# Attention and expert block on one core: unit 15's scores, mask and exponential take other places in their engines' orders

## The reference

```
x = x + attention(layernorm(x))     # 16 heads of 64, causal, with a second layernorm inside
x = x + experts(layernorm(x))       # encoder, router, 2 of 8 experts, decoder, layernorm
```

```
scores = jnp.where(causal, einsum('bqhe,bkhe->bhqk', q, k) * scale, -inf)
z = einsum('bhqk,bkhe->bqhe', softmax(scores, axis=-1), v)
attn_out = einsum('bqhe,hed->bqd', z, W_o) + b_o
```

## Time and profile before

| what | us |
|---|---|
| median of 3 runs | 1162.31 |
| the runs | 1160.6 to 1169.64 |
| the profiled execution, its time | 1161.35 |
| its span, first to last instruction | 1159.6 |
| busy in it: TensorE, VectorE, ScalarE, GpSimd | 1033.9, 861.9, 739.5, 743.9 |
| one attention step, 414.20 to 443.31 | 29.11 |

### The profile page before, as it was taken

One profiled execution on the slowest core, in us unless ns is written; L12 is line 12 of the kernel. 1 busy time (PEld: TensorE's weight loads), 2 busy tenths in 40 slices (PEclk: granted clock), 3 DMA queues, 4 the chain that ended last, 5 costly groups with the idle time before them and its releaser, 6 DMA issues.

```text
span 1159.6 us, 51488 instructions
## 1 busy us (share of the span) xinstructions
PE 1033.9 (89%) x19852; PEld 768.7 (66%) x19852; DVE 861.9 (74%) x2047; ACT 739.5 (64%) x1540; POOL 743.9 (64%) x728
## 2 busy tenths in 40 slices
PE   5789999999999999999999999999999978899984
PEld 2567777777777777777777777777777766454542
DVE  7877777777777777777777777777777786357563
ACT  4656666666666666666666666666666655667663
POOL 5786666666666666666666666666666633344544
PEclk8999999999999999999999999999999998899998
DMA  7678877777777777777777777777777773131322
GB/s 172 160 192 210 195 181 186 184 185 186 183 183 187 187 182 188 185 184 184 185 185 184 186 183 184 186 183 186 184 183 186 188 149 76 38 83 47 91 59 51
DMA packets 131599, 188.79 MB, mean 163 GB/s; under 512 B 46576, under 2 KB 57840, under 8 KB 131568
## 3 DMA queue, kind: packets, MB, share of 16 engines
q1 hardware_dynamic: 131568, 188.40, 67.9%
HBM read 133.39 MB, written 21.36 MB: 133 GB/s over the span
## 4 chain that ended last, share of the span: by engine, by line
PE 65%; POOL 13%; issue 8%; DVE 6%; ACT 5%; DMA 1%; POOLq 1%; DVEq 0%; ACTq 0%; SPq 0%
PE ZB L714 27%; PE SPS L697 13%; PE SPS L698 10%; POOL QS L495 6%; PE ZB L687 5%; POOL X L520 3%; POOL QS L493 3%; ACT RAW L1279 2%; ACT OT L1316 1%; PE SPS L849 1%; PE SPS L875 1%; PE ZB L681 1%; PE ZB L890 1%; PE ZB L884 1%; ACT PRL L1299 1%
## 5 line engine op out<-in xcount | busy, mean ns | idle before, releaser
L1018 DVE CUSTOM_DVE_ANT_0 SSB<-SPS,MASK 128x640 f32<-128x640 f32 (+7 forms) x512 | 375.1, 751 | 174.5 <-PE SPS L698 163.6
L714 PE MATMUL ZB<-PTZ,VR 32*64 32x256 f32 (+2 forms) x16384 | 321.5, 294 | 30.9 <-ACT RAW L1279 23.7
L697 PE MATMUL SPS<-KHP,QS 128*128 (+2 forms) x768 | 323.5, 427 | 23.9 <-DVE NM L1018 19.5
L1299 ACT ACTIVATE PRL<-SSB,NM 128x640 f32<-128x640 f32 (+3 forms) x256 | 253.1, 989 | 128.4 <-DVE NM L1018 128.0
L714 PEld LDWEIGHTS ZB<-PTZ,VR 32*64 32x64 f32 x16384 | 271.8, 131 | 77.7 <-issue 63.1
L698 PE MATMUL SPS<-KLP,QS 128*128 (+2 forms) x768 | 259.7, 348 | 0.0
L981 DVE STREAM_TRANSPOSE PTZ<-PRL 128x640 f32<-128x640 f32 (+3 forms) x256 | 257.6, 1026 | 0.0
L1299 ACT ACTIVATE PRS<-SSB,NM 128x128 f32<-128x128 f32 (+3 forms) x256 | 142.6, 558 | 139.8 <-DVE NM L1018 139.5
L697 PEld LDWEIGHTS SPS<-KHP,QS 128*128 128x128 f32 x768 | 145.3, 189 | 99.3 <-issue 45.8
L495 POOL TENSOR_TENSOR QS<-RAW,QS 64x512 fp32r<-64x512 f32 x128 | 165.0, 1289 | 10.3
L514 POOL TENSOR_TENSOR PTZ<-PTZ,RSB 128x512 f32<-128x512 f32 x64 | 81.2, 1291 | 139.6 <-ACT PTZ L1310 139.3
(11 more groups left out here) (170 smaller groups left out, 1053.4 us busy)
## 6 DMA issues: line engine op xcount, KB each, us to landing
VR<-v_scratch SPq DMA_DIRECT2D x256, 256.0 KB, 6.8
KHP<-KHP SPq DMA_DIRECT2D x64, 256.0 KB, 3.2
KLP<-KLP SPq DMA_DIRECT2D x64, 256.0 KB, 3.8
v_scratch<-V SPq DMA_DIRECT2D x32, 512.0 KB, 7.0
RSB<-rcp_scratch SPq DMA_DIRECT2D x64, 256.0 KB, 3.9
XTB<-xt_scratch SPq DMA_DIRECT2D x62, 256.0 KB, 4.4
XW<-xt_scratch SPq DMA_DIRECT2D x30, 512.0 KB, 7.4
VR<-gate_scratch SPq DMA_DIRECT2D x16, 512.0 KB, 5.9
```

What stands on the lines that cost most here:

```text
L697: pe.matmul(SP_[n % 2][:, c0:c0 + wc], q, kh[:, c0:c0 + wc], start=True, stop=False)
L714: last = pe.matmul(ZB[h * DH:(h + 1) * DH, i, kt * TR:QT * TR], VR[rows, j, kt, h * DH:(h + 1) * DH], turned_block(h, kt, j, rows), start= ...
L1018: v.tensor_tensor_reduce(out=SSB[n % 2][:, 0:w], in0=SP_[n % 2][:, 0:w], in1=MASK[:, S - w:S], scale=1.0, scalar=BIG, op0=ALU.add, op1=ALU ...
L1299: act.activation(exps_of(n), SSB[n % 2][:, 0:w], ACT.Exp, bias=NM[:, col:col + 1], scale=-1.0, accum_out=L[:, col:col + 1]).then_inc(exp_d ...
```

## The change

It concerns three places in the seam. TensorE makes scores 15 behind both output products and no longer ahead of them. VectorE takes mask 15 behind turn 12, and in the next step mask 0 ahead of turn 13. ScalarE takes OT0 ahead of exponential 14, OT1 ahead of exponential 15, and exponential 15 itself only in the next step, behind projection 0's evacuation (in the last step at the step's end). No instruction is added or taken away, and GpSimd's and SyncE's orders are as they were.

```diff
@@ pe_step
             v_of(1)
-            scores(14, 15)
+            scores(14)
             out_of(0)
             out_of(1)
+            scores(15)
@@ dve_step
-            turn_back(13)
             mask(0)
             if first:
                 mask(1)
                 norm_late(v, 1)
+            turn_back(13)
             turn_back(14)
...
             mask(14)
+            turn(12)
             mask(15)
-            turn(12)
@@ act_step
                 qk(0)
+                act_exp(act, it - 1, 1 - par, UNITS - 1)
                 exps_to(0, 1)
...
             v_of(1)
+            out_of(0)
             exps_to(14, 15)
-            out_of(0)
-            exps_to(15, 16)
             out_of(1)
+            if last:
+                act_exp(act, it, par, UNITS - 1)
```

## The result

The changed kernel takes 1127.08 us (median of 4 runs, 1124.21 to 1129.44) against 1161.45 for the kernel before: a ratio of 0.969, with a 95% interval from 0.964 to 0.975, so 34.4 us less. Forecast were 1119.2 us and a range from 1112 to 1140. The execution that was profiled is the fastest of the four, 1124.21 us with a span of 1122.5; the span became 37.1 us shorter.

What follows compares the result with a forecast made beforehand. TensorE bounds the step's middle; the gain lies in the seam, the last 9.25 us. 1161.35 - 43.8 + 0.5 + 0.15 = 1118.2 us profiled, 0.96 below the median, so 1119.2 us; range 1112 to 1140.

Steps and rivals of the forecast that it cites:

- The start of the gain: ScalarE at the seam: OT0 starts at 434.35 in place of 435.91, 1.56 us earlier.
- The three lines: Seam, start of value products: VectorE allows 441.56, ScalarE 441.71, GpSimd 441.75 (441.85 at half of the seams).
- the loop's branch: TensorE, branch now behind scores 15: bounded by 0 and 0.6 us, taken as 0; mask 2's slack nil on VectorE's line.
- 1.51 us a seam: Each full seam: value products start at 441.80 instead of 443.31; bounds 1.2 to 1.7 us.
- 43.8: All 29 full seams together: 1.51 us times 29 saved; bounds 35 to 49 us.
- +0.5: Last seam, no projection: mask 15 starts 1.55 later, less turn 12's 1.05, so 0.5 us lost.
- 0.15 more: End of attention: later mask 15 against earlier copy of the second output product; +0.15 us, between 0 and +0.5.
- The two rules weighed: ScalarE table switches (2.57 or 5.4 us a seam) and TensorE's loop branch (0 to 0.6 us); neither in the sum.
- B: Seam: VectorE or ScalarE becomes the end, 0.5 to 1 us later than worked out; 1141 us; chance 0.16.
- C: Seam: later mask 15 costs what the earlier OT0 gives, so gain hidden; 1162 us; chance 0.05.
- D: ScalarE: exponential 15 stuck behind projection 0 if XTB's DMA is late; slower, 1191 us for one us; chance 0.04.
- E: ScalarE: table loads at 2.57 us a seam, value products 1.0 later; slower, 1191 us; chance 0.01.

Runs made afterwards that it cites:

- e1: Changed kernel with TensorE's order put back: scores 14 and 15 ahead of both output products; 1142.68 us, ratio 0.984 to the kernel before.
- e6: Changed kernel with TensorE's scores 2 ahead of projection 3; 1117.45 us, ratio 0.962 to the kernel before.
- e8: Kernel of e6 with scores 15 between the two output products instead of behind both; 1114.83 us, ratio 0.961 to the kernel before.
- e5: Changed kernel with exponential 15 between OT1 and projection 0's evacuation, at the end of its own step; 1127.63 us, ratio 0.971 to the kernel before.
- e4: Changed kernel with exponential 15 back ahead of OT1 on ScalarE; 1172.36 us, ratio 1.010 to the kernel before.
- e2: Changed kernel with mask 15 again ahead of turn 12 on VectorE; 1164.35 us, ratio 1.003 to the kernel before.
- e7: Kernel of e2 with scores 2 made four times and scores 4 twice in the 30 middle steps; 1149.63 us, ratio 0.989 to the kernel before.

## Why the prediction was right, and by what it was off

**What bounds the kernel and where the gain lies: right.** TensorE kept the middle of the step, and the seam gave all of it.

**The start of the gain: right.** OT0 came 1.66 us earlier (forecast 1.56), because its input was released a little faster than the 0.3 us that I put. e1 shows that this start is the end of a race with GpSimd as its next runner, and that it takes both ScalarE's and TensorE's new order.

**The three lines: GpSimd's and ScalarE's right, VectorE's 0.5 us too short.** GpSimd's last subtraction ended at 452.20 (440.57) and ScalarE's three evacuations began at 450.92 (439.29) and ended at 453.09 (441.46), against 439.23 and about 441.5 forecast. For VectorE I took the length of the line from the first seam and only wrote of mask 2's input that its slack was nil, in the paragraph on the loop's branch. That term of the sum was mis-sized. In the first seam scores 2 were early; in a full seam TensorE issues four projections and three score units from 436.0 on, and I never laid out their ends. At 0.86 us for a projection and 0.23 for a narrow score unit, scores 2 are issued until 451.81 (440.18), while VectorE would have taken them at about 440.0. The wait of 0.34 us, with 0.17 more along VectorE's line than the first seam has, put the value products at 442.07 and not at 441.56. The term "1.51 us a seam" measured 1.20 in this seam and 1.215 as the mean of 28 steps, so "43.8" was 35.2, 8.6 us less. e6 takes away this wait by one move, and its 28 steps are 9.5 us shorter together than the changed kernel's, its median 9.6. Of the further 0.17 no run says where it comes from.

**The small terms.** The profiled execution was forecast at 1118.2 us and took 1124.21, 6.0 more. From the value products of the first full seam to those of the last full seam, 93.78 to 909.31 before and 90.85 to 872.35 after, the kernel saved 34.03 us in 28 steps, 8.3 less than 28 times 1.51. From there to the last seam's value products, at 936.58 before and 900.16 after, it lost 0.54: the +0.5 of the forecast was right. The first full step saved 2.75, 1.2 more than a seam was to give; two stalls of TensorE's that the chain calls issue, 1.04 and 2.03 us, are not there in the new execution, which waits in that step for GpSimd and a DMA in their place. I hold this for start-up, and no run was made on it. The end of attention and the experts' part took 0.68 less, where I had put 0.15 more; this was not followed up, and what lies behind the last full seam differs by 5.5 us between e6 and e8. The start of the kernel gave another 0.18. So about 2 us that no one worked out in advance covered a part of the 8.3.

The median of the changed kernel is 7.9 us above the forecast 1119.2, and so 1.9 more than these 6.0, because its profiled execution lies 2.87 below its median where I had added 0.96. At 1127.08 it is just inside the forecast's bracket of 1114 to 1128, and that it is inside owes something to those 2 us; the range as a whole, up to 1140, did not need them.

**The two rules weighed: neither cost anything.** The price that the Trainium skill, "ScalarE: Activation LUTs", section "Table sets: the hidden batching unit", gives for switching table sets never fell due: exponential 15 follows projection 0's evacuation by 0.68 us with no load between, and in both kernels the exponentials' line has two table loads in the whole execution. The loop's branch behind scores 15 shows no gap either (the last matmul of scores 15 is issued at 447.42, the first of the projection at 447.66).

**The rivals.** B, VectorE's line ending later than worked out, is what happened, with the seam 0.3 us late and not the 0.5 to 1 that I priced; that is small enough to stay within the forecast's bracket. C did not come. D, exponential 15 stuck behind projection 0, did not come, and e5 shows that its place there is not even needed; e4 shows the reverse case, OT1 stuck behind exponential 15, which does make the kernel slower. E is excluded by the rows.

## What to carry to other kernels

When several lines race to the same point, lay out each engine's whole queue through the new seam, the one that "only changes its order" included; a line measured elsewhere is only as good as the inputs it had there. Moving a producer later is paid for unless every wait on it moves behind the work that others need: the mask behind the turn, the exponential behind the copy. And when the last line is found, look for a single instruction ahead of it that nobody needs yet: projection 3 here, worth another 10 us. When the lines are level, as in e8, a further move gives nothing.

## What the runs showed of the hardware that I had not expected

A little idle time on TensorE can cost more than itself. e2's order adds 0.54 us to a step, and behind 16 of its 29 full seams the granted clock fell at the next burst of matmuls, at 1.68 us each time. TensorE had been busy for 1.50 of the 3 us ahead both where the clock fell and where it stayed at 1.00, so what these 3 us held does not settle by itself whether it falls. In the seam of the kernel before TensorE was busy for 1.74 of them and in that of the changed kernel for 2.11, and the clock stayed at 1.00 behind every full seam of both. The kernel before shows such a fall in its last seam:

```profile
931.58:936.58 5.00, 1.50 (x7) 0.92 (x7) 4.97 (x14) 3.14 (x10) 4.29 (x5) 1.00 0.94 241
936.58:941.77 5.19, 5.19 (x129) 4.57 (x129) 3.58 (x23) 1.20 (x4) 1.99 (x2) 0.67 0.15 29
```

The changed kernel has it there too: 5.01 us for the same 128 matmuls, from 900.16 on.

The Trainium skill, "TensorE: Matmul & The Clock Gate", section "Part 1: The HAM clock gate (the "warmup" mystery)", says that the lower clock is the default and that activity releases it. The runs agree: e7 puts needless matmuls into the gap and is 14.7 us faster than e2.
